# Self-attention's input projections as three products of 16-bit halves, the weights split during the cross-attention

## What is computed

```python
# layer 1: cross-attention, 16 heads of 32, 8192 keys in each batch
q, k, v = x @ Wq, context @ Wk, context @ Wv
x = x + softmax(q k^T / sqrt(32), mask) v @ Wo
# layer 2: causal self-attention over 512 tokens, 16 heads of 32
q_amp, k_amp = softplus(x @ Wq_amp.T), softplus(x @ Wk_amp.T)          # rms-normalised per head
q_phi, k_phi = pi * tanh(x @ Wq_phi.T), pi * tanh(x @ Wk_phi.T)
scores = (q_amp cos(q_phi)) (k_amp cos(k_phi))^T + (q_amp sin(q_phi)) (k_amp sin(k_phi))^T
x = x + softmax(scores * exp(log_scale) / sqrt(32), causal) (x @ Wv.T) @ Wo.T
# layer 3: 16 experts, the best 2 for each token, capacity-limited
x = x + experts(x)
```

## Time and profile before

| | before |
|---|---|
| median of 3 runs | 2142.18 us |
| the profiled execution's own time | 2142.47 us |
| its span, first to last instruction | 2140.7 us |
| cross-attention's steps | to about 1573 us |
| self-attention | about 1573 to 1980 us |
| experts | about 1980 to 2141 us |
| TensorE busy | 1966.8 us, 92% |
| VectorE busy | 1748.2 us, 82% |
| ScalarE busy | 1512.3 us, 71% |
| granted TensorE clock, mean | 0.969 |

### The profile page before, as it was taken

The page is one execution under the profiler, slowest core; times in us unless marked ns, Lnnn a source line. Parts: engine busy times, 40 slices in busy tenths (PEclk is TensorE's granted clock), DMA queues, the critical chain, the costliest instruction groups (busy, mean ns, idle before and its releaser), DMA issues.

```text
span 2140.7 us, 30896 instructions
## 1 busy us (share of the span) xinstructions
PE 1966.8 (92%) x11354; PEld 794.9 (37%) x11354; DVE 1748.2 (82%) x1657; ACT 1512.3 (71%) x1918; POOL 44.3 (2%) x58
## 2 busy tenths in 40 slices
PE   7799999999999998999999999999888999985493
PEld 3233333333333333333333333333224444443382
DVE  5589999999999998799999999999975676665244
ACT  2388888888888886688888888888843555552020
POOL 2000000000000000000000000000000000000203
PEclk9899999999999999999999999999999999998697
DMA  5533323333233332133323333223300000021884
GB/s 189 190 104 94 90 79 89 89 94 94 75 89 91 92 101 87 50 90 89 94 75 94 90 89 99 75 84 77 131 21 1 1 1 1 1 89 32 283 280 143
DMA packets 112586, 194.55 MB, mean 91 GB/s; under 512 B 10288, under 2 KB 63536, under 8 KB 112432
## 3 DMA queue, kind: packets, MB, share of 16 engines
q1 hardware_dynamic: 109872, 184.12, 29.2%
q0 software_dynamic: 2560, 8.39, 1.2%
HBM read 108.58 MB, written 50.33 MB: 74 GB/s over the span
## 4 chain that ended last, share of the span: by engine, by line
PE 80%; DVE 8%; issue 4%; DMA 4%; ACT 2%; POOL 1%; SPq 1%; POOLq 0%; ACTq 0%; DVEq 0%
PE ps L964 21%; PE ps L1082 20%; PE ps L882 11%; PE ps L879 11%; PE ps L989 5%; PE ps L1145 3%; DVE dacc L1483 2%; PE ps L1017 2%; PE ps L952 1%; PE ps L1155 1%; DMA kscr<-wsm 1%; PE ps L995 1%; PE ps L1045 1%; PE ps L1030 1%; DMA kst<-kscr 1%
## 5 line engine op out<-in xcount | busy, mean ns | idle before, releaser
L1319 ACT ACTIVATE pt<-ps,bias 128x1024 f32<-128x1024 f32 x1024 | 1109.4, 1114 | 222.5 <-PE ps L1082 221.3
L1483 DVE TENSOR_TENSOR dacc<-dacc,pt 128x2048 f32<-128x2048 f32 x504 | 1152.9, 2288 | 49.0 <-ACT pt L1319 22.9
L1082 PE MATMUL ps<-qst,kst 128*128 128x512 f16 x2048 | 615.1, 383 | 19.8 <-ACT pt L1319 19.0
L964 PE MATMUL ps<-pt,vt 128*32 128x512 f32 x4096 | 495.4, 601 | 0.0
L1082 PEld LDWEIGHTS ps<-qst,kst 128*128 128x128 f16 x2048 | 178.3, 98 | 423.9 <-ACT pt L1319 131.3
L879 PE MATMUL ps<-wsm 128*128 128x512 f16 x1152 | 315.0, 384 | 14.8 <-DVE wsm L1440 10.8
L882 PE MATMUL ps<-wsm 128*128 128x512 f16 x1152 | 310.8, 380 | 5.5 <-ACT vt L1200 2.9
L964 PEld LDWEIGHTS ps<-pt,vt 128*32 128x32 f32 x4096 | 107.1, 109 | 263.6 <-issue 243.1
L879 PEld LDWEIGHTS ps<-wsm 128*128 128x128 f16 x1152 | 113.5, 99 | 157.8 <-issue 10.8
L882 PEld LDWEIGHTS ps<-wsm 128*128 128x128 f16 x1152 | 112.4, 98 | 145.2 <-issue 4.2
L1284 ACT ACTIVATE pr<-ps,nmx 128x128 f32<-128x128 f32 (+3 forms) x128 | 66.4, 523 | 117.0 <-DVE nmx L1585 116.7
(11 more groups left out here) (186 smaller groups left out, 1250.6 us busy)
## 6 DMA issues: line engine op xcount, KB each, us to landing
kscr<-wsm SPq DMA_DIRECT2D x128, 256.0 KB, 3.5
kst<-kscr SPq DMA_DIRECT2D x128, 256.0 KB, 3.4
kst<-kst SPq DMA_DIRECT2D x128, 256.0 KB, 3.4
wsm<-in_ctx SPq DMA_DIRECT2D x32, 768.0 KB, 4.7
qst<-qscr SPq DMA_DIRECT2D x32, 128.0 KB, 2.9
xbuf<-xn SPq DMA_DIRECT2D x16, 256.0 KB, 6.6
wsm<-in_gate SPq DMA_DIRECT2D x8, 512.0 KB, 5.0
wsm<-in_fc SPq DMA_DIRECT2D x8, 512.0 KB, 5.9
```

Source lines behind the costliest of these rows:

```text
L964: p = e.matmul(ps[32 * h:32 * h + 32, 4 + n % 2, :], vt[:, kb % 2, ch, c:c + 32], pt[:, (2 * i + h // 2) % 6, h % 2, :], start=ch == 0, st ...
L1082: p = e.matmul(ps[:, 2 * half + h2, :], kst[:, kb % 2, h, ch * 128:ch * 128 + 128], qst[:, h, :], start=True, stop=True)
L1319: e.activation(pt[:, (2 * i + half) % 6], ps[:, 2 * half:2 * half + 2, :], ACT.Exp, bias=bias[:, 4 * kb + ch:4 * kb + ch + 1], scale=SCORE ...
L1483: e.tensor_tensor(own_heads, own_heads, probs, ALU.add).then_inc(S["add"], 1)
```

## The change

The five weights of layer 2 are scaled by `WS` = 64 and split into 16-bit halves while the cross-attention runs, in 20 pieces of 128x512 (four for each weight), one to a key block: blocks 1 to 13 and 17 to 23. For each piece SP loads 256 KB of float32 into `dn_[:, 0]` at step 9, ScalarE writes the high half into `whalf` (in `dn_[:, 1]`) at step 12, VectorE the rest at step 15, and SP stores 256 KB to a scratch tensor in HBM at step 1 of the next block. At step 496 the five weights come back as halves, in as many bytes as before.

Each projection is then 12 products of 16 bits in place of 4 of float32: for each of four chunks high x high, high x rest, rest x high. An event is six 16-bit products. The transposed tile is split too: ScalarE's copy writes the high half with a factor 16, and VectorE has a new piece `low` for the rest. The factor comes out again in the readers of PSUM (`UNIT`). `amp` becomes two pieces on VectorE: `relu` reads PSUM, and `amp` adds in SBUF.

Beside this a `memset` moves ahead of `bias` on VectorE, some semaphores share a name, and some buffers lie elsewhere in SBUF.

```diff
+XS = 16.0
+UNIT = 1.0 / (XS * WS)
+CHUNKS = [(c, xi, wi) for c in range(4) for xi, wi in ((0, 0), (0, 1), (1, 0))]
+SPLITS = {kb: divmod(j, 4) for j, kb in enumerate((*range(1, 14), *range(17, 24)))}
+WEIGHTS = ("wqa", "wka", "wqp", "wkp", "wv2")
...
     def p23(t, n):
-        out.append(("p23", t, 2 * n, 2 * n + 2, fill((2 + n // 2,)) if n % 2 == 0 else ()))
+        out.append(("p23", t, 6 * n, 6 * n + 6, fill((2 + n // 2,)) if n % 2 == 0 else ()))
...
-        elif slot == 3:
+        if slot == (3 if begun else 2):
+            out.append(("relu", t))
+        if slot == 3:
             out.append(("amp", t))
...
             if t < 7:
                 out.append(("copy", t + 1))
+                out.append(("low", t + 1))
...
+        wscr = nc.dram_tensor("wscr", [5, 128, 2, 4, 512], F16).ap()
+        whl = wf_.bitcast(F16).rearrange("p (a b c d) -> p a b c d", a=5, b=2, c=4)
+        whalf = dn_[:, 1].bitcast(F16).rearrange("p (a b) -> p a b", a=2)
@@ sp @@
-                    for w, n in enumerate(("wqa", "wka", "wqp", "wkp", "wv2")):
-                        e.dma_start(wsm[:, w], A[n].rearrange("(k p) n -> p k n", p=128)).then_inc(S["ws"], 16)
+                    e.wait_ge(S["wst"], 16 * 20)
+                    for n in range(5):
+                        e.dma_start(whl[:, n], wscr[n]).then_inc(S["ws"], 16)
+                if i % 16 == 1 and kb - 1 in SPLITS:
+                    n, k = SPLITS[kb - 1]
+                    e.wait_ge(S["wlo"], 4 * n + k + 1)
+                    e.dma_start(wscr[n, :, :, k, :], whalf).then_inc(S["wst"], 16)
+                if i % 16 == 9 and kb in SPLITS:
+                    n, k = SPLITS[kb]
+                    if n or k:
+                        e.wait_ge(S["wlo"], 4 * n + k)
+                    if kb > 15:
+                        e.wait_ge(S["att"], 4)
+                    e.dma_start(dn_[:, 0], A[WEIGHTS[n]][128 * k:128 * k + 128, :]).then_inc(S["wld"], 16)
@@ pe @@
-                    for m in range(lo, hi):
-                        n, k = m // 4, m % 4
-                        p = e.matmul(ps[:, w0 + n, :], xT2[:, t % 2, k * 128:k * 128 + 128], wsm[:, w0 + n, k, :],
-                                     start=k == 0, stop=k == 3)
+                    for m in range(lo, hi):
+                        n, (c, xi, wi) = m // 12, CHUNKS[m % 12]
+                        p = e.matmul(ps[:, b0 + n, :], xT2[:, t % 2, xi, c * 128:c * 128 + 128], whl[:, w0 + n, wi, c, :],
+                                     start=m % 12 == 0, stop=m % 12 == 11)
@@ act @@
-                    e.activation(xT2[:, i, :], ps[:, 0, :], ACT.Copy).then_inc(S["xTs"], 1)
+                    e.activation(xT2[:, i, 0], ps[:, 0, :], ACT.Copy, scale=XS).then_inc(S["xTh"], 1)
-                    e.activation(t1[:], pair(0), ACT.Abs).then_inc(S["act"], 1)
+                    e.activation(t1[:], pair(0), ACT.Abs, scale=UNIT).then_inc(S["mag"], 1)
@@ act @@
+                if i % 16 == 12 and kb in SPLITS:
+                    n, k = SPLITS[kb]
+                    e.wait_ge(S["wld"], 16 * (4 * n + k + 1))
+                    if n or k:
+                        e.wait_ge(S["wst"], 16 * (4 * n + k))
+                    e.activation(whalf[:, 0], dn_[:, 0], ACT.Copy, scale=WS).then_inc(S["whi"], 1)
@@ dve @@
+            e.memset(att[:, 0, :], 0.0)
             e.wait_ge(S["maxs"], 4)
...
-            e.memset(att[:, 0, :], 0.0).then_inc(S["zeros"], 1)
...
-                    e.scalar_tensor_tensor(out=amp[:, i, :], in0=pair(0), scalar=0.0, in1=t1[:], op0=ALU.max,
-                                           op1=ALU.add).then_inc(S["amp"], 1)
+                    e.wait_ge(S["dve"], relu)
+                    e.tensor_tensor(amp[:, i, :], amp[:, i, :], t1[:], ALU.add).then_inc(S["amp"], 1)
+                elif what == "relu":
+                    e.wait_ge(S["mag"], t + 1)
+                    e.tensor_scalar(amp[:, i, :], pair(0), UNIT, 0.0, ALU.mult, ALU.max).then_inc(S["dve"], 1)
+                elif what == "low":
+                    e.wait_ge(S["xTh"], t + 1)
+                    e.scalar_tensor_tensor(out=xT2[:, i, 1], in0=ps[:, 0, :], scalar=XS, in1=xT2[:, i, 0], op0=ALU.mult,
+                                           op1=ALU.subtract).then_inc(S["xTs"], 1)
@@ dve @@
+                if i % 16 == 15 and kb in SPLITS:
+                    n, k = SPLITS[kb]
+                    e.wait_ge(S["whi"], 4 * n + k + 1)
+                    e.scalar_tensor_tensor(out=whalf[:, 1], in0=dn_[:, 0], scalar=WS, in1=whalf[:, 0], op0=ALU.mult,
+                                           op1=ALU.subtract).then_inc(S["wlo"], 1)
+                if i == STEPS - 1:
+                    self_piece(("low", 0))
                 adds(i)
```

More of the change, by code:

```diff
@@ L188, in pe @@
         p.then_inc(f["pe"], 1)
-        e.wait_ge(f["act"], s_b.at("act", 0, 1))
+        e.wait_ge(f["dve"], s_b.at("dve", 0, 2))
         for w0 in (0, 2):
-            for m in range(8):
-                n, k = w0 + m // 4, m % 4
-                p = e.matmul(ps[:, n, :], xT2[:, 0, k * 128:k * 128 + 128], wsm[:, n, k, :], start=k == 0, stop=k == 3)
+            for m in range(24):
+                n, (c, xi, wi) = w0 + m // 12, CHUNKS[m % 12]
+                p = e.matmul(ps[:, n, :], xT2[:, 0, xi, c * 128:c * 128 + 128], whl[:, n, wi, c, :], start=m % 12 == 0,
+                             stop=m % 12 == 11)
             p.then_inc(f["pe"], 1)
@@ L259, in dve @@
                         ALU.mult).then_inc(f["dve"], 1)
+        e.wait_ge(f["act"], s_b.at("act", 0, 1))
+        e.scalar_tensor_tensor(out=xT2[:, 0, 1], in0=ps[:, 0, :], scalar=XS, in1=xT2[:, 0, 0], op0=ALU.mult,
+                               op1=ALU.subtract).then_inc(f["dve"], 1)
         end(e)
@@ L548 @@
 SEMS = """const
- wk wv x0 x1 wq mask late zero wo2
- c0 c1 qw0 qw1 qw2 qw3 ql0 ql1 ql2 ql3 kw0 kw1 kw2 kw3 kr0 kr1 kr2 kr3 ku0 ku1 ku2 ku3 ws
+ wk wv x0 x1 wq late zero wo2
+ c0 c1 qw0 qw1 qw2 qw3 qx0 qx1 qx2 qx3 kw0 kw1 kw2 kw3 kr0 kr1 kr2 kr3 ku0 ku1 ku2 ku3 ws wld whi wlo wst
  pool dve act hi0 chi lo0 wsplit split var root norm n1 xt xTc qry qlo unit khi klo vev maxs max1 bias esl
- sc ex add av oac fin dnc dnx okr att prj x2 flagm flag zeros
- xn turn xTs p01 abs amp p23 p4 sv ms mroot msr phi tabs sin cos polar qkT QT KT
+ sc ex add av oac fin dnc dnx okr att prj x2 flagm flag
+ xn turn xTh xTs p01 mag abs amp p23 p4 sv ms mroot msr phi tabs sin cos polar qkT QT KT
  score nmx prob scale pT tcD tcA value aT wom x3 lvar lroot lstat xn3 rT rC rM lg
  e0 e1 e2 e3 e4 e5 e6
- lgs pexp ohb cum dst sct0 xl0 xl1 xl2 xl3 eT xeT up sgx hT dn oe os0 os1 y out
+ lgs pexp ohb cum dst sct0 eT xeT up sgx hT dn oe os0 os1 y out
 """.split()
@@ L765, in sp @@
             e.dma_start(wo, A["wo"].rearrange("(k p) n -> p k n", p=128)).then_inc(S["late"], 16)
-            e.wait_ge(S["zeros"], 1)
+            e.wait_ge(S["bias"], 1)
             for i in range(16):
@@ L979, in self_piece @@
                     p.then_inc(S["turn"], 1)
-                elif what in ("p01", "p23"):
+                elif what in ("p01", "p23", "p4"):
                     lo, hi = ev[2], ev[3]
-                    w0 = 2 if what == "p23" else 0
+                    w0, b0, end = {"p01": (0, 0, 24), "p23": (2, 2, 24), "p4": (4, 1, 12)}[what]
                     e.wait_ge(S["xTs"], t + 1)
@@ L987, in self_piece @@
                     for m in range(lo, hi):
-                        n, k = m // 4, m % 4
-                        p = e.matmul(ps[:, w0 + n, :], xT2[:, t % 2, k * 128:k * 128 + 128], wsm[:, w0 + n, k, :],
-                                     start=k == 0, stop=k == 3)
-                    if hi == 8:
+                        n, (c, xi, wi) = m // 12, CHUNKS[m % 12]
+                        p = e.matmul(ps[:, b0 + n, :], xT2[:, t % 2, xi, c * 128:c * 128 + 128], whl[:, w0 + n, wi, c, :],
+                                     start=m % 12 == 0, stop=m % 12 == 11)
+                    if hi == end:
                         p.then_inc(S[what], 1)
[L993 to L998, removed]
                 elif what == "qkT":
```

55 lines of the change are left out of this document (28 added, 27 removed).

## The result

The changed kernel took 2155.62, 2155.62, 2156.71 and 2153.85 us, a median of 2155.62 us; the kernel before took 2141.37 us on the same chips. The ratio is 1.0059, 95% interval 1.0047 to 1.0072: 0.6% slower, where 0.7% was forecast. The profiled execution took 2155.62 us with a span of 2153.9 us, 13.2 more than before.

What follows compares the result with a forecast made beforehand. TensorE was taken to set the pace in the cross-attention and most self-attention slots. 2142.5 + 32.4 (blocks) + 0.5 (memset) - 18.9 (self-attention) = 2156.5 us, 0.7% slower; range 2137 to 2181.

Steps and rivals of the forecast that it cites:

- The load's place and its landing: Cross-attention, 20 blocks: load issued where the context load stood, on average 1.08 us before ScalarE asks, landing in 3.4 us.
- the load lands early: Rival, cross-attention: with a landing of 2.0 us ScalarE hardly waits, total 2128.5 us; chance 0.20.
- The wait and what is absorbed: Cross-attention step 12: ScalarE waits 2.3 us a block, 0.7 absorbed; cost 1.62 us a block, 32.4 us for 20.
- The rest of the piece at nothing: Cross-attention: VectorE's rest, the store, the delayed context load and the loads at step 496 cost nothing.
- `p23` and `p01`, less `relu` and `low`: Self-attention: shorter projection events gain 12.3 and 10.6 us; VectorE's `relu` costs 2.8 us and `low` 3.2 us.
- a falling clock: Rival, cross-attention: TensorE's clock falls during the waits in a third to half of 20 blocks, total 2172 us; chance 0.08.
- `p4` as nothing: Self-attention slots 6 and 7, tiles 1 to 7: 14 shorter events gain nothing, TensorE's wait only grows.
- VectorE takes the self-attention's gain: Rival, self-attention: `relu` and `low` lie wholly on the path, gain only about 5 us, total 2170 us; chance 0.12.
- The memset: VectorE, moved ahead of `bias`, for which all wait: 0.5 us of cost.
- The handover: Transposes of tile 0 to first score product: `p4` of tile 0 and `p01` of tile 1 gain 2.0 us; `low` covered.

Runs made afterwards that it cites:

- e1: The changed kernel with ScalarE's copy of the piece's high half behind step 14 instead of step 12; 2124.51 us, ratio to the kernel before 0.9918.
- e2: The changed kernel with SP's load of the piece in step 1 instead of step 9; 2124.36 us, ratio to the kernel before 0.9920.
- e4: The changed kernel with float32 self-attention as before, without `low` and `relu`, pieces still prepared but unused; 2170.28 us, ratio to the kernel before 1.0140.
- e5: e1 plus eight 16-bit products nobody reads ahead of the first `p4` event of tiles 1 to 7; 2121.64 us, ratio to the kernel before 0.9912.
- e3: The changed kernel with ScalarE's copy of the piece's high half behind step 11 instead of step 12; 2258.0 us in one run.

## Why the prediction was right

The direction, the size and the main mechanism were right; term by term it was less even.

- *The load's place and its landing.* Right. It went out where the context load had stood and landed in 3.2 to 3.6 us, 3.36 on average, with 3.4 forecast. So the rival "the load lands early" falls. The estimate of 2.6 us by the Trainium skill, "DMA: Bandwidth & Descriptors", section on the anatomy of one DMA, was too short here. The section gives its formula for DMAs on the GpSimd path, which the prediction left out, and these loads went out on SP's hardware queue.
- *The wait and what is absorbed.* The wait was 2.06 us in place of 2.3, and 0.77 of it was absorbed in place of 0.7, so the blocks cost 25.7 us in place of 32.4. The landing was right, so the quarter of a microsecond lies in the timing of SP against ScalarE, taken from the old trace: SP issued the load 1.33 us before ScalarE asked for it, on average, in place of 1.08. Why is open.
- *The rest of the piece at nothing.* Right, shown by e1 and e2, where the blocks are at 45.04 us with all of it in.
- *`p23` and `p01`, less `relu` and `low`.* 22.9 less 6.0, 16.9 us, was forecast for the score stretch. Measured were 14.4 against the kernel before and 12.0 against e4. What is missing is the low clock: e5, in which slots 8-9 are not hit, has 314.7 us, 18 less than e4 and 6.0 less than the changed kernel. Of these 6.0 about 1 us each stands in slots 8 to 11 of turns 1, 2, 5 and 6, and most of the rest in turn 7, where the clock was low too. The prediction had looked for a falling clock in the wrong stage, and had counted `p4` as nothing when in its place it cost something: less work in front of a wait made the wait longer. The rival "VectorE takes the self-attention's gain" falls with the same numbers, as 14.4 of the forecast 16.9 us were gained.
- *The memset.* The forecast 0.5 us can't be told apart. The first context split starts at 106.3 us in place of 105.5, but at 103.5 to 107.0 in the variants, which all have the same memset.
- *The handover.* This term failed. I had counted 2.0 us gained there, and `low` of tile 0 as covered by the last value products. Measured were 1.3 us lost. TensorE's timeline:

```profile
1600.16 2.75 PE L1016 MATMUL ps<-wsm,xT 128*128 128x512 f16 x12 [1.51 <-DVE xT L1571]
...
1618.08 1.08 PE L1005 MATMUL ps<-ident,xn 128*128 128x128 f32 x4 [4.74 <-DVE xn L1559]
1618.96 5.54 PE L979 MATMUL ps<-xn 128*128 128x512 f32 x8
```

  `low` of tile 0 queues behind an addition of 2.28 us on VectorE, and TensorE waits 1.51 us for it. Then TensorE, done early with the cheaper `p23`, waits 4.74 us in place of 0.69 for the flag check and `relu`, and the next eight records take 5.54 us in place of 3.60. Of the 4.74 us the new `relu` is 1.23. A further 1.35 is VectorE's idle time behind the flag check, 5.08 us in place of 3.73; it is 3.96 to 5.08 in the variants, and no experiment touched it. Over 1616 to 1624 us the granted clock was 0.57:

```profile
1616.00:1624.00 8.00, 5.92 (x12) 3.05 (x13) 5.49 (x7) 4.33 (x4) 0.00 (x0) 0.57 0.02 8
```

  In the profiles of e1 and the variants built on it the handover takes 46.5 to 48.8 us, against 46.8 in the one profile before, so the sign of the term is not certain; that the 2.0 us were not gained is clear.
- *The end.* 1.7 us more there, with nothing changed: the stretch varies from one execution to the next.
- *The sum.* The blocks were overestimated by 6.7 us, and the gains by 5.8 (16.9 and 2.0 in place of 14.4 and -1.3). The memset's 0.5 us, the end and the steps outside the 20 blocks (1.1 us shorter) add about nothing. The two errors nearly cancelled, which is why the total of 2156.5 fell within a microsecond of 2155.62. Part of that closeness is luck.

## What to carry to other kernels

Before a load is put into a DMA queue "at step 9", look at when that queue gets there: what an in-order queue issues behind two full waits goes out when those have landed, and the consumer's step has to be chosen from that moment and the landing time, not from the loop index. With the consumer two steps later, or the load eight steps earlier, the same change is 0.8% faster than the kernel before instead of 0.6% slower (e1, e2; e5 0.9%). And where TensorE waits for another engine anyway, making its work shorter gave nothing here, and the longer wait cost something behind it.

## What was not expected of the hardware

- A wait may cost more than it lasts. 5.1 us of ScalarE's wait cost 6.5 us a block, with the mean granted clock at 0.97, where 2.06 us of wait cost 1.29, with the clock at 1.00. The low stretches stand in all 20 blocks of e3 and in none of the changed kernel's.
- 1.7 us of products that nobody reads, in front of a wait of TensorE, made the score stretch 3.0 to 3.6 us shorter (two profiles each of e5 and e1). The projection behind the wait took 1.88 us, where in turns with a low clock it had taken 3.17.
